# Edge-free tiles of a four-layer graph network by threes: the third layer made in turned stripes that are the fourth layer's input

## The reference, cut to what matters

```python
h = jnp.maximum(_layernorm(x), 0.0)
x = x + gat(gat(h, W1, ...) -> relu, W2, ...)          # layers 1, 2
h = jnp.maximum(_layernorm(x), 0.0)
# layers 3, 4: gcn_conv(x, W, b):
h = x @ W
deg = segment_sum(ones_like(dst), dst);  norm = rsqrt(deg)[src] * rsqrt(deg)[dst]
out = segment_sum(h[src] * norm[:, None], dst) + b      # self-loops included
x = x + gcn(relu(gcn(h, W3, b3)), W4, b4)
```

## Time and profile before

| what | value |
|---|---|
| median of 3 runs (lowest to highest) | 2167.13 us (2159.16 to 2168.96) |
| the profiled execution | 2162.97 us, span 2161.0 us, mean granted TensorE clock 0.995 |
| busy: PE, DVE, ACT, POOL | 2119.0, 1461.1, 952.0, 868.0 us |
| chain that ended last, by engine | PE 82%, DVE 7%, POOL 5%, issue 3% |
| largest single line of the chain | L1005 (`products`), 71% |

### The profile page before, as it was taken

The page is one execution under the profiler, slowest core; times in us unless marked ns, Lnnn a source line. Parts: engine busy times, 40 slices in busy tenths (PEclk is TensorE's granted clock), DMA queues, the critical chain, the costliest instruction groups (busy, mean ns, idle before and its releaser), DMA issues.

```text
span 2161.0 us, 35596 instructions
## 1 busy us (share of the span) xinstructions
PE 2119.0 (98%) x13151; PEld 1336.0 (62%) x13151; DVE 1461.1 (68%) x3322; ACT 952.0 (44%) x1289; POOL 868.0 (40%) x1067
## 2 busy tenths in 40 slices
PE   7999999999999999999999999999999999999997
PEld 4666665556666666666666666666666666666654
DVE  8989754435776675434989898664666667876563
ACT  4444454444454554443544454334343333333332
POOL 3221167614332321344554543542534322255462
PEclk9999999999999999999999999999999999999999
DMA  5988999995555559998655556666866647775552
GB/s 184 235 224 200 227 218 197 212 224 170 192 174 198 197 180 244 230 218 218 214 191 203 186 194 212 238 244 204 301 229 230 223 175 261 243 245 180 175 189 86
DMA packets 297490, 451.99 MB, mean 209 GB/s; under 512 B 193267, under 2 KB 193465, under 8 KB 297190
## 3 DMA queue, kind: packets, MB, share of 16 engines
q1 hardware_dynamic: 256950, 277.12, 46.1%
q0 software_dynamic: 40368, 172.60, 25.6%
HBM read 234.94 MB, written 179.89 MB: 192 GB/s over the span
## 4 chain that ended last, share of the span: by engine, by line
PE 82%; DVE 7%; POOL 5%; issue 3%; ACT 1%; DMA 1%; SPq 0%; POOLq 0%; DVEq 0%; ACTq 0%
PE ps_h L1005 71%; PE ps_z L981 5%; POOL meta_rows L690 3%; PE ps_e L1081 1%; PE ps_e L1082 1%; DVE edge_mem L1274 1%; PE ps_e L1071 1%; PE ps_e L1072 1%; DVE z_lo L1234 1%; DVE bn L1170 1%; POOL rstd L699 1%; DMA rows<-row_out 0%; DMA edge_mem<-meta_rows 0%; ACT z L884 0%; DVE pre L1196 0%
## 5 line engine op out<-in xcount | busy, mean ns | idle before, releaser
L1005 PE MATMUL ps_h<-w_hi,z_hi 128*128 128x384 f16 x2508 | 614.3, 327 | 1.6 <-DVE w_lo L1160 1.6
L1005 PE MATMUL ps_h<-w_lo,z_hi 128*128 128x384 f16 x2508 | 614.4, 327 | 0.0
L1005 PE MATMUL ps_h<-w_hi,z_lo 128*128 128x384 f16 x2508 | 614.0, 327 | 0.0
L1005 PE MATMUL ps_h<-w_hi,x_keep 128*128 128x384 f16 x2568 | 526.3, 326 | 2.7 <-issue 2.7
L871 ACT ACTIVATE row_out<-ps_h,grow 128x768 f32<-128x768 f32 x237 | 212.9, 898 | 624.7 <-PE ps_h L1005 615.1
L1234 DVE TENSOR_TENSOR z_lo<-ps_z,z_hi 128x768 f16<-128x768 f32 x209 | 199.4, 954 | 227.1 <-ACT z_hi L876 226.8
L1005 PEld LDWEIGHTS ps_h<-w_hi,x_keep 128*128 128x128 f16 x2568 | 249.9, 98 | 166.3 <-issue 3.6
L1005 PEld LDWEIGHTS ps_h<-w_lo,z_hi 128*128 128x128 f16 x2508 | 245.7, 98 | 163.1 <-issue 1.4
L1005 PEld LDWEIGHTS ps_h<-w_hi,z_lo 128*128 128x128 f16 x2508 | 245.7, 98 | 163.0 <-issue 1.3
L1005 PEld LDWEIGHTS ps_h<-w_hi,z_hi 128*128 128x128 f16 x2508 | 245.3, 98 | 154.2 <-issue 21.2
L1005 PE MATMUL ps_h<-w_lo,x_keep 128*128 128x384 f16 x1284 | 313.8, 326 | 0.0
(11 more groups left out here) (224 smaller groups left out, 2550.1 us busy)
## 6 DMA issues: line engine op xcount, KB each, us to landing
rows<-row_out SPq DMA_DIRECT2D x199, 384.0 KB
rows<-e_out SPq DMA_DIRECT2D x60, 384.0 KB, 4.5
row_in<-in_x SPq DMA_DIRECT2D x40, 384.0 KB, 4.2
row_in<-rows SPq DMA_DIRECT2D x40, 384.0 KB, 4.5
x_rows<-pre SPq DMA_DIRECT2D x40, 384.0 KB, 3.6
res<-x_rows SPq DMA_DIRECT2D x40, 384.0 KB, 4.0
pure_rows<-row_out SPq DMA_DIRECT2D x39, 384.0 KB
row_in<-pure_rows SPq DMA_DIRECT2D x39, 384.0 KB, 4.5
```

Of the source, the lines that this page charges most:

```text
L1005: last = nc.tensor.matmul(ps_h[s][:, a, 0:HALF], zp[:, c, :], wp[:, c, a * HALF:(a + 1) * HALF], start=(c == 0 and zp is zh and wp is hi), ...
```

## The change

The 39 pure tiles' layers 3 and 4 are taken in 13 batches of three tiles: three "stripes" of layer 3, then three tiles of layer 4.

- A stripe (`stripe`) takes weights as the stationary side and the three turned tiles as the moving one: two chunks m of 128 output channels by 384 nodes, six chunks c and three products each, so 36 products of 128x384. Its result lies with channels on partitions, as layer 4 wants its input: `evict_stripe` (ScalarE) writes it twice with relu, bias and scale (float32 into `z4_f`, float16 into `z4_hi`), `low_stripe` (VectorE) writes the rest into `z4_lo`.
- The 39 layer-4 tiles lose their `prepare_even`, `make_z`, turn, `upper_parts` and `low_parts`. One bounded scale for all of them is worked out once (`chain_scales`).
- The three layer-3 inputs are still prepared, made and turned, into `z3_hi` and `z3_lo`, one buffer each of 384 columns. A list `Q` beside `T` says in which window each is turned (`turn_at`): those of a batch whose predecessor is near go into the windows of the predecessor's first two layer-4 tiles and into the one before the batch; else into the three before the batch, where a source or mixed tile is turned as well. A second turn of a window is put behind `side_step(1)`, its `upper_parts` and `low_parts` at the end of that window's queue.
- Order by that rule: part 3 is five times (4 source tiles, batch), windows 158 to 207; 3m is 208 to 227; part 4 is 7 sources, batch, 7, batch, 6, batch, 228 to 265; 4m 266 to 285; part 5 is five batches, 286 to 315. Two turns fall in windows 159, 160, 232, 233, 283 and 284.
- `plain_at` takes every (7j)//5-th window instead of every (3j)//2-th. Layer 4's weights are split one window earlier.

```diff
@@ order_of_tiles
+    def put_batch():
+        b, g = count[0], len(seq)
+        count[0] += 1
+        follows = b > 0 and seq[g - 1].chain
+        last = [t.g for t in seq if t.chain and t.layer == 4][-THREE:]
+        turns = [last[0], last[1], g - 1] if last and b > 0 and last[1] >= g - 12 else [g - 3, g - 2, g - 1]
+        rows = [Tile(None, 3, b * THREE + k, turn_at=turns[k], batch=b, part=k) for k in range(THREE)]
+        preps.extend(rows)
+        for k in range(THREE):
+            seq.append(Tile(len(seq), 3, None, turn_at=-9, batch=b, part=k))
+        for k in range(THREE):
+            seq.append(Tile(len(seq), 4, rows[k].pos, turn_at=-9, batch=b, part=k))
+            seq[-1].of = rows[k]
...
-    part("3", 3, 0, chains[0], range(PURE, FREE))
+    part("3", 3, batches[0], range(PURE, FREE))
...
-    CHAINS = (14, 10)
+    BATCHES = (PURE // THREE - 8, 3, 5)
...
-    plain_at = {begin["4"] + 4 + (3 * j) // 2: j for j in range(ET)}
+    plain_at = {begin["4"] + 4 + (7 * j) // 5: j for j in range(ET)}
@@ scalar
             def upper_parts(t):
                 act.wait_ge(z_turned, t.tn + 1)
-                wait(act, h_ready, t.g - 1)
-                nc.scalar.activation(pair3(z_hi[t.slot]), psum_pair(ps_z), ACT.Copy).then_inc(z_hi_ready, 1)
+                if t.chain:
+                    if t.batch > 0:
+                        act.wait_ge(stripe_ready, t.batch * KC)
+                    to = z3_hi[:, :, t.part * P:(t.part + 1) * P].rearrange("p (a c) n -> p a c n", a=2)
+                    nc.scalar.activation(to, psum_pair(ps_z).rearrange("p a (c n) -> p a c n", n=P), ACT.Copy).then_inc(z3_hi_ready, 1)
...
+            def evict_stripe(t):
+                act.wait_ge(chain_ready, 1)
+                for a in range(2):
+                    m = 2 * t.part + a
+                    n = t.batch * KC + m
+                    act.wait_ge(stripe_ready, n + 1)
+                    if n >= 2:
+                        act.wait_ge(z4_lo_ready, n - 1)
+                    nc.scalar.activation(z4_f[a], ps_h[t.slot][:, a, 0:HALF], ACT.Relu, bias=b3_turned[:, 1, m:m + 1], scale=chain_sc[:, 4:5])
+                    last = nc.scalar.activation(z4_hi[:, m, :], ps_h[t.slot][:, a, 0:HALF], ACT.Relu, bias=b3_turned[:, 1, m:m + 1],
+                                                scale=chain_sc[:, 4:5])
+                    last.then_inc(z4_hi_ready, 1)
@@ tensor
+                ago = turned_tiles[t.tn - 1]     # turn(t): ps_z must be free
+                    if ago.chain:
+                        pe.wait_ge(z3_lo_ready, ago.c + 1)
+                    else:
+                        pe.wait_ge(z_lo_ready, ago.hn + 1)
...
+                    if t.chain and t.part == 0:  # products(t), chunk c
+                        pe.wait_ge(z4_lo_ready, t.batch * KC + c + 1)
...
+            def stripe(t, side_step):
+                pe.wait_ge(z3_lo_ready, (t.batch + 1) * THREE)
+                rows_kept(t)
...
+                for a in range(2):
+                    m = 2 * t.part + a
+                    for c in range(KC):
+                        for wp, zp in ((hi, z3_hi), (lo, z3_hi), (hi, z3_lo)):
+                            last = nc.tensor.matmul(ps_h[t.slot][:, a, 0:HALF], wp[:, c, m * P:(m + 1) * P], zp[:, c, :],
+                                                    start=(c == 0 and zp is z3_hi and wp is hi),
+                                                    stop=(c == KC - 1 and zp is z3_lo))
+                        if c == KC - 1:
+                            last.then_inc(stripe_ready, 1)
+                        if (a, c) in ((0, 3), (1, 1)):
+                            side_step(a)
...
                 def side_step(k):
+                    if k == 1:
+                        for t in turned[1:]:
+                            turn(t)
@@ vector
+            def low_stripe(t):
+                for a in range(2):
+                    m = 2 * t.part + a
+                    dve.wait_ge(z4_hi_ready, t.batch * KC + m + 1)
...
+                    V.tensor_tensor(z4_lo[:, m, :], z4_f[a], z4_hi[:, m, :], ALU.subtract).then_inc(z4_lo_ready, 1)
+            def chain_scales():
+                dve.wait_ge(bias_loaded[3], 16)
+                sc = chain_sc
+                for m in range(KC):
+                    step(V.tensor_tensor_reduce(e_prod[:, 0:P], bias_bc[3][:, m * P:(m + 1) * P], ident[:, :], 1.0, 0.0, ALU.mult, ALU.add,
+                                                b3_turned[:, 0, m:m + 1]))
...
             def window(w):
                 gat = gat_of(w)
                 t = tile(w, -1)
                 if t and t.layer == 4:
                     result(t)
+                if t and t.layer == 3 and t.chain:
+                    low_stripe(t)
+                turned = [t for t in due(w) if not t.crossed]
+                for t in turned[:1]:
                     low_parts(t)
...
-                t = tile(w, 3)
-                if t and not t.crossed:
+                for t in due(w + 2):
                     (prepare_first if t.layer == 1 else prepare_third if t.layer == 3 else prepare_even)(t)
...
+                for t in turned[1:]:
+                    low_parts(t)
@@ main loop of vector
+                if w == max_at[4] + 2:
+                    chain_scales()
```

More of the change, by code:

```diff
@@ L63, in __init__ @@
         self.by_pool = layer == 2 or (mixed and layer > 2)
-APART = 5
 FIRST_CROSSED = 6
 SECOND_CROSSED = 124
[L71 to L79, removed]
-        begin[name] = len(seq)
[L81 to L92, removed]
+THREE = 3
@@ new lines, in order_of_tiles, with put, part @@
+def order_of_tiles(NT, PURE, FREE, batches):
+    seq, preps, begin = [], [], {}
+    count = [0]
+    def put(layer, pos, mixed=False):
+        t = Tile(len(seq), layer, pos, mixed)
+        seq.append(t)
+        preps.append(t)
+    def put_batch():
[11 more added lines that the diff above has]
+            seq[-1].of = rows[k]
+    def part(name, layer, n, sources):
+        begin[name] = len(seq)
+        done = 0
+        for i, pos in enumerate(sources):
+            put(layer, pos)
+            while done < n and (i + 1) * n >= (done + 1) * len(sources):
+                put_batch()
+                done += 1
+        while done < n:
+            put_batch()
+            done += 1
@@ L496, in rows_free @@
         def rows_free(e, t):
-            ago = next((p for p in reversed(T[:t.g]) if p.loaded and p.in_slot == t.in_slot), None)
+            ago = next((p for p in reversed(Q[:t.pn]) if p.in_slot == t.in_slot), None)
             if ago is not None:
@@ L719, in load @@
                 if t.layer == 3:
-                    ago = next((p for p in reversed(T[:t.g]) if p.layer == 3 and (t.x - p.x) == 2), None)
+                    ago = next((p for p in reversed(Q[:t.pn]) if p.layer == 3 and (t.x - p.x) == 2), None)
                     if ago is not None:
@@ L856, in evict @@
             def evict(t):
-                act.wait_ge(h_ready, t.g + 1)
-                if t.g >= 2:
-                    ago = T[t.g - 2]
+                act.wait_ge(h_ready, t.hr + 1)
+                ago = next((p for p in reversed(T[:t.g]) if p.slot == t.slot and (p.layer == 4 or not p.chain)), None)
+                if ago is not None:
                     if ago.stored:
@@ L1030, in window @@
             def window(w):
-                t = tile(w, 1)
-                if t and not t.crossed:
+                turned = [t for t in due(w) if not t.crossed]
+                for t in turned[:1]:
                     turn(t)
@@ L1058, in window @@
                 if t := tile(w, 0):
-                    products(t, side_step)
+                    (stripe if t.layer == 3 and t.chain else products)(t, side_step)
                 if w - 1 in rank_at:
@@ L1525, in window @@
                         edge_max(layer, now)
-                t = tile(w, 3)
-                if t and not t.crossed:
+                for t in due(w + 2):
                     (prepare_first if t.layer == 1 else prepare_third if t.layer == 3 else prepare_even)(t)
-                t = tile(w, 4)
-                if t and t.crossed:
-                    (prepare_first if t.layer == 1 else prepare_even)(t)
                 if w in rank_at:
```

286 lines of the change are left out of this document (165 added, 121 removed).

## The result

The changed kernel takes 2176.62 us in the median (20 runs, lowest 2170.25) where the kernel before, run beside it, takes 2165.5 (20 runs, 2158.96 to 2171.73): the ratio is 1.0054, 95% interval 1.0041 to 1.0066. So it is 0.5% slower, by 11 us, and lies just above my range (2127 to 2176); the forecast was 2159. One of the 20 runs (2243.03 us), and later the profiled one of *exact* (2244.78 us), had a mean granted clock of 0.94 where the others have 0.99; the ratios are taken without them. The profiled execution took 2181.63 us, its span 2179.5 against 2161.0 of before.

The account below looks back on a forecast made before the run. TensorE, 98% busy, was taken as the bound, with VectorE's lateness making it stand. Part 3 +8.6, part 4 −4.0, 4m +6.9, part 5 −16.6 gave −5.1 us: 2158, stated as 2159, range 2127 to 2176.

Parts of the forecast that it names:

- The removed turns and the stripes: Parts 3 to 5: 39 turns go, 25.7 us of TensorE; stripe products keep their pace at zero cost.
- the rival of 7 us: Stripes: changing the stationary side costs 7 us, 2166 in all; chance 0.10, shared with something between.
- Part 5 and 4m: Part 5: turns and waits of the sums go, −16.6 us; end of 4m: stands and clock in 283, +6.9.
- the sum: Whole kernel: part 3 +8.6, part 4 −4.0, end of 4m +6.9, part 5 −16.6, together −5.1 us.
- The bunching of part 3: Part 3: grouped VectorE preparations and results make TensorE stand 5.1 us a cycle, 20.4 in four cycles.
- The clock: Low clock behind waits of 2.2 to 3.5 us: 1.0 net per part 3 cycle, 4.0 in all; 1.9 in 283.
- The double turn in 159: Window 159, start of part 3: second turn waits for VectorE's `low_parts`, stands of 1.6 and 1.5, 3.1 us.
- the splitting of layer 4's weights: One window earlier than before: costs nothing, since TensorE has no wait there.
- Window 232: Part 4's double turn: stand of 0.8, then 1.1 for a sum waiting on ScalarE's carry, 1.9 us.
- The spacing of the sums: Layer 3's sums at the new `plain_at`: costs nothing, since TensorE has no wait there.
- the third, compounding stands: Part 3 and 4m: low clock follows each stand over 2 us, norm at its upper bound; +14, 2178; chance 0.16.
- the upper bound of the norm: Part 3, window 169: late GpSimd norm delays ScalarE's weights, stand of 1.5 to 3 us, 2.2 taken in the forecast.

Follow-up runs that it names:

- exact: Changed kernel with the first six third-layer inputs of the chains waiting only for the crossed tile whose buffer they take over: 2174.73 us, ratio 1.0031.
- after: The changed kernel itself in its first profile, against the kernel before: profiled execution 2181.63 us, median of runs 2176.62 us.
- its repeat: The changed kernel, unchanged, profiled a second time: part 3 took 382.47 us, part 4 276.16, 4m 136.86, part 5 209.42.
- far: Changed kernel with batches whose predecessor is far also turned in the predecessor's free windows, one turn each in 232, 233, 283, 284: 2165.59 us, ratio 0.9984.
- plain: Changed kernel with the steps of layer 3's sums put back to every (3j)//2-th window: 2173.95 us, ratio 1.0031.
- ownslot: Changed kernel with the `pre` buffers of source and mixed tiles numbered by a counter of their own, not shared with chain tiles: 2177.73 us, ratio 1.0037.
- three: Changed kernel with the edits of far, plain and ownslot together: 2162.07 us, ratio 0.9958.

## Why the prediction was wrong, point by point

**The removed turns and the stripes: right.** 39 turns gone, products at 326 ns, stationary side and single bank at no cost; the rival of 7 us falls.

**Part 5 and 4m: right.** No wait of the sums over 0.2 us is left in part 5, which is 17.6 us shorter (said 16.6). In 4m the stand in 283 is 3.35 (said 3.5), with the low clock behind it, 1.6 (said 1.9); the next turn waited 0.2 where I had 1.5. The milestones hold 1.3 of turns moved into 4m, so 5.6 of stands and clock stand against 6.9 in the sum, and 16.3 against 16.6 in part 5:

```profile
1937.09 1.51 PE L1043 MATMUL ps_z<-ident,z 128*128 128x128 f32 x6 [3.35 <-DVE z_lo L1333]
1938.40 0.85 PE L1080 MATMUL ps_h<-w_hi,z_hi 128*128 128x384 f16 x2
1939.04 0.85 PE L1080 MATMUL ps_h<-w_lo,z_hi 128*128 128x384 f16 x2
```

**The bunching of part 3: mechanism right, size near, detail off.** I had 20.4 us of stands, 5.1 a cycle; the excess of TensorE's starts over their pace at the weights' transposes adds up to 18.5. The row of window 167, VectorE's result and `low_parts` ahead of the maximum (timeline of after):

```profile
1103.87 0.95 DVE L1373 TENSOR_TENSOR res<-row_out,x_keep 128x768 f32<-128x768 f32 x1
...
1105.73 0.95 DVE L1333 TENSOR_TENSOR z_lo<-ps_z,z_hi 128x768 f16<-128x768 f32 x1
...
1107.43 0.15 DVE L1421 TENSOR_SCALAR e_negmax<-e_max 128x1 f32<-128x1 f32 x1
...
1107.93 0.28 ACT L999 ACTIVATE e_self<-lrelu,e_negmax 128x1 f32<-128x1 f32 x1
1108.26 0.48 PE L1161 MATMUL ps_e<-ident,rank_mem 128*128 128x128 f32 x1 [3.04 <-ACT e_self L999]
```

3.04 where 2.9 was said. One of 0.7 at the end of window 165 was not foreseen, and 169's was 1.66 (said 2.2) where the clock had stayed high, and 0.3 or less where it had not. With the clock high a cycle so has 5.9 us of stands.

**The clock: right as a net price.** I took 1.0 a cycle net, 4.0 in all. Gross, from TensorE's starts behind those stands against their pace elsewhere, it is 7.5: 3.0 and 2.9 in two cycles, 1.6 in one, 0 in the third. Here are four stretches of 5 us in after (columns: start and end, length, busy time of PE, PEld, DVE, ACT, POOL, then the granted TensorE clock, DMA share, GB/s). The first, third and fourth lie behind three equal waits of 3.03 to 3.04 us, the second is an undisturbed one:

```profile
1108.00:1113.00 5.00, 4.74 (x17) 3.01 (x18) 4.86 (x9) 2.09 (x5) 3.32 (x3) 0.50 0.84 284
1116.00:1121.00 5.00, 5.00 (x35) 3.29 (x34) 4.79 (x12) 3.28 (x5) 3.72 (x3) 1.00 0.69 236
1186.90:1191.90 5.00, 4.99 (x18) 3.16 (x19) 4.86 (x9) 1.88 (x3) 3.32 (x3) 0.50 0.88 279
1265.50:1270.50 5.00, 5.00 (x29) 3.29 (x30) 4.86 (x9) 1.77 (x3) 3.33 (x4) 1.00 0.86 278
```

0.50 is the 1.2 GHz level; in the first two cycles it lasts for some 6 us, where the earlier trace rows had six pairs of products (3.9 us), and the third time it didn't come. What I set against it, that the stand of 169 is given back, came in full. From window 161 to 171 and so on, the first three cycles of six traces (after, its repeat, *far*, *plain*, *ownslot*, *three*) take 77.6 to 77.8 us, whether there was no low clock behind the stand of 3.04 us or one of some 3 us (16 cycles); only where it lasted some 6 us, twice in after, they take 78.7 and 78.6. In the fourth cycle it is the same, 112.9 us from window 191 on in four traces and 113.8 to 113.9 in the two with 6 us (the two turns that *far* and *three* moved there taken off). So the net price in after is some 2.0 us, below my 4.0 and inside the bounds. Stands and clock of the four cycles together are 26.0 us against the 24.4 of the sum.

**The double turn in 159: the first step that failed, too small by 5.** Said 3.1 in all and no clock; it is 6.0 of stand, 0.7 at the two next turns and 1.5 of clock, 8.1. The step that failed is VectorE's queue ahead of `low_parts`: I left out its wait for the store out of a shared `pre` (3.25 us). Taking that away brought only 0.7 to 1.6 back; the two stands that were left, 5.2 against 3.1, say that VectorE's lateness there was some 2 us more than I reckoned. The `w_lo` of 1.01 us ahead of `low_parts` in the rows above may be part of it: I had put the splitting of layer 4's weights at nothing because TensorE had no wait there before. No run takes it away alone.

Part 3's miss is that and the cycles: 5.0 (159) + 1.6 = 6.6, against 15.3 − 8.6 = 6.7.

**Window 232: the second step that failed, too small by 6.** I had 0.8 and 1.1. The timeline of after:

```profile
1564.57 0.63 POOL L737 TENSOR_SCALAR veps<-mv 128x1 f32<-128x1 f32 x1
...
1566.31 1.03 ACT L940 ACTIVATE z<-x_keep,nmr,rstd 128x768 f32<-128x768 f32 x1 [4.12 <-POOL nmr L741]
...
1567.47 0.96 DVE L1289 TENSOR_TENSOR x_keep<-row_in,row_x 128x768 f32<-128x768 f32 x1 [1.81 <-ACT z L940]
...
1572.51 0.95 DVE L1333 TENSOR_TENSOR z_lo<-ps_z,z_hi 128x768 f16<-128x768 f32 x1
1572.72 0.95 POOL L725 DMA_INDIRECT edge_mem<-rows,pos_src  x1 [0.30 <-issue]
...
1573.60 0.85 PE L1043 MATMUL ps_z<-ident,z 128*128 128x128 f32 x6 [2.81 <-DVE z_lo L1333]
...
1575.33 0.18 POOL L737 TENSOR_SCALAR veps<-mv 128x1 f32<-128x1 f32 x1
...
1576.62 1.03 ACT L940 ACTIVATE z<-x_keep,nmr,rstd 128x768 f32<-128x768 f32 x1 [6.98 <-POOL nmr L741]
1576.76 1.62 PE L1178 MATMUL ps_e<-edge_mem,rank_mem 128*128 128x385 f32 x2 [2.31 <-issue]
```

TensorE stands 2.81 and 2.31 and then runs at the low clock for some 2.8 us more, 8.1 in all with the drains. VectorE had the statistics at 1570.7, but GpSimd is busy with four gathers of the first sums and gets to the norm at 1575.33; that is the second stand. The first has the same cause a window earlier: the statistics were there at 1561.6, GpSimd came to them at 1564.57 behind gathers too, `make_z` was late, and VectorE's next preparation stood 1.81 us for it, ahead of the `low_parts` that the turn wanted. I had looked for that chain in part 5, and not here, where sums begin in the window of a double turn.

**The spacing of the sums: put at nothing.** It costs 2.8 us at 1685 in after, with the drain (1.2 to 2.6 of wait in six traces). With 5.9 of turns saved: −5.9 + 8.1 + 2.8 = +5.0, against 5.3 measured; I had −4.0.

These three steps make 14.0 of the 15.9 us between my −5.1 and the +10.8 of the traces (5.0, 6.2 and 2.8); the rest is +1.6 of the cycles, +0.9 of layer 2, which I hadn't in the sum, and −1.0 of part 5.

**The rivals.** The truth is close to the third, compounding stands (2178), in its time alone, and that by luck: the waits of a cycle sum to 3.7 to 5.4 us, not 7.5, the upper bound of the norm didn't come, and its price, the clock in part 3, came at 2.0 net and not at 4 × 2.9. The miss lies at the double turns of 159 and 232 and at the sums, where no rival had more than the forecast. (That rival also names 10.6 us for 4m in its text and adds 8.8 in its sum.) The Trainium skill ("TensorE: Matmul & The Clock Gate", section "HAM oscillation — how this bites in real kernels") describes a kernel in which the product bursts behind long waits for transfers each begin at the low clock. These traces agree in part: it followed 35 of 45 waits of 3 us and more, and also 22 of 31 of the shorter ones between 2 and 3 us.

## What to carry to other kernels

Taking work out of the bounding engine pays only what the order of the other queues lets through: here 25.7 us of transposes went and came back as stands, because steps that had alternated were put in groups; putting other tiles between them made each period 1.8 us shorter. Lay a period out engine by engine. A stand of over 2 us can cost up to twice its length by the clock, but where another late step follows it in the period, most of that is given back (0 to 1.1 us net of up to 3.0 here). Look at the places outside the period apart: there the layout failed, and the three pairs of double turns cost 21.8 us (8.1, 8.1, 5.6), nearly as much as the four cycles' 26.0. And repeat a profile before reading a difference of 2 us out of it.

## What the runs showed of the hardware

I had not expected the clock to be so uneven at one and the same stand. Behind the 3.03 to 3.04 us wait at the end of window 167 and its counterparts (four in each of after, its repeat, far, plain, ownslot and three, 24 in all) the pairs of products start 0.64 us apart 17 times, and 7 times not. Over twelve of the traces (all but *exact*), behind the start-up: of 70 waits between 1 and 2 us none brought the low clock by itself, of 31 between 2 and 3 us 22 were followed by it (both counted where two stood within 5 us), of 45 of 3 us and more 35. In the 24 the low clock lasted some 3 us 13 times and cost the cycle nothing that its length shows, and some 6 us four times, which cost 0.9 to 1.1.
